# Graph attention passes of a GNN: values made beside the keys, selections made by VectorE, banks as accumulators

## The chip, the cores and the metric

The kernel runs on one core of a Trainium2 chip. The metric is the device time of one execution in microseconds; the kernel before takes 12023.37 us, the median of three runs from 12015.92 to 12034.72. The core has a matmul engine (TensorE, PE in profile rows; its weight loads are PEld), VectorE (DVE), ScalarE (ACT), GpSimd (POOL) and SyncE (SP), which only issues transfers and waits. Each runs its own instruction stream; they meet at semaphores.

## The reference, cut to what matters

Four graph layers run one after the other on 5000 nodes, 80000 edges sorted by destination, and width 128, all in float32. The first layer (`_L0_gnn_ref`) runs three times and holds all that is changed here:

```python
x_i = x[dst]
x_j = x[src] + edge_attr
q = (x_i @ wq.T + bq).reshape(-1, HEADS, DH)
k = (x_j @ wk.T + bk).reshape(-1, HEADS, DH)
v = (x_j @ wv.T + bv).reshape(-1, HEADS, DH)
alpha = jnp.sum(q * k, axis=-1) / jnp.sqrt(jnp.float32(DH))
a = softmax of alpha over the edges of one destination
out = jax.ops.segment_sum(a[..., None] * v, dst, num_segments=N)
```

The layer's remainder (a dense block, a GRU cell, norms) and the other three layers (neighbour sums with a two-layer net, four rounds of typed neighbour sums with a GRU, one more attention layer) are not touched.

## The kernel before, in words

Edges are taken in tiles of 128, nodes in 40 blocks of 128. A *step* is a pair (edge tile, node block) that the tile's destinations touch; there are 672 steps, planned at the start of the program (`step_tables`, lines 321 to 537: VectorE computes tables with one small operation after another, SyncE sends them through DRAM to where they are read into registers). Four steps make a *region* (`GROUP`), four regions a turn of a hardware loop (`REGIONS`, 42 turns). So a pass has 168 regions. `select` holds for a step a 128x128 matrix of zeros and ones: edge e belongs to node n of the block.

Each of the three rounds of the first layer has, among others:

- `gat_score_pass` (lines 986 to 1111). GpSimd gathers the rows `x[src]` of a region with four indirect DMAs (`gathers_by_step`, line 832; a gather may start once the region four places back is turned, `p_turned`). SyncE loads the edges' own rows into `attr`, four DMAs. VectorE builds `select` (line 862, edges down the partitions) and adds gathered rows and edge rows (line 1059). TensorE turns both: four transposes of `select` (line 1091), four of the sum (line 1093). ScalarE copies the two turned banks to SBUF (`spread`, line 1039; `mixT`, line 1040). SyncE stores `mixT` in DRAM (`rows_dram`, line 1024) for the value pass. TensorE makes the keys, `mixT` times `wk` (line 1105), and brings each edge the query of its destination, `spread` times the block's queries (line 1108). ScalarE copies the keys (line 1048), VectorE multiplies, sums by head and adds a bias term (lines 1068, 1073, 1076). Leads, in regions: VectorE's select and sum two ahead, TensorE's turning one ahead. PSUM: one bank each for the turned select and the turned sum, keys and queries with two buffers each.
- `gat_softmax`, not touched.
- `gat_value_pass` (lines 1113 to 1235). SyncE loads `rows_dram` back, one DMA for a region. TensorE makes the values from it with `wv` (line 1220). The selection is made by GpSimd (a difference, line 1144) and ScalarE (absolute value, line 1158, and 1 minus it, cut at zero, line 1161). VectorE weighs the values with the softmax weights (line 1171). TensorE sums the edges of each node (line 1231), and VectorE adds each step's 128x132 result to the accumulators in SBUF, steps by turns to `acc` and `t1` (lines 1188, 1190); at the end one addition joins the two (line 1212).

Other passes of the program matter for the rows below: `sum_pass` (lines 898 to 984) gathers by edge tile with a ring of 16 regions and sums in PSUM banks that are never copied in between; its banks are cleared first by eight matmuls (line 982).

## Time and profile before

| | us |
|---|---|
| median of three runs | 12023.37 |
| the profiled execution's own time | 12019.95 |
| its span, first to last instruction | 12018.1 |
| PE busy | 6550.1 |
| PEld busy | 5479.0 |
| POOL busy | 6209.6 |
| DVE busy | 4612.7 |
| ACT busy | 2251.5 |

Busy times are sums over the whole program, and the engines take turns in setting the pace, so they are read by stage: a window of the trace for each pass, then the groups of instructions and the waits in it. "Idle before" is the time that an engine sat idle ahead of a group's instructions; a releaser is what ended it ("issue": nothing that the profile shows; "remote": an event that it does not tie to an instruction).

### The profile page before, as it was taken

The numbers are of one execution on the slowest core, as the hardware profiler recorded it, in microseconds if no ns is written. First come the engines' busy times: TensorE is split into PE (matmuls) and PEld (weight loads), VectorE is DVE, ScalarE is ACT, GpSimd is POOL, SyncE is SP. The second block draws the span as 40 slices with busy tenths as digits, with TensorE's granted clock in tenths as the row PEclk, the third lists the DMA queues.
The fourth block names the chain that finished last, engine by engine and source line by source line (L and its number), as shares of the span: only waits on it lengthen the run. The fifth ranks groups of instructions, "written<-read, shape, count | busy, mean of one in ns | idle before, by whom it ended". The sixth has DMA issues, their size and how long they took to land. (4 is left out here: it accounts for less than half of the span.)

```text
span 12018.1 us, 148393 instructions
## 1 busy us (share of the span) xinstructions
PE 6550.1 (55%) x36272; PEld 5479.0 (46%) x36273; DVE 4612.7 (38%) x10118; ACT 2251.5 (19%) x4313; POOL 6209.6 (52%) x6365
## 2 busy tenths in 40 slices
PE   3666786566786665884335334433533443365555
PEld 3555665555765555853323223233323322244443
DVE  4444754444754444752113112211311221135555
ACT  1222552222542222641000000000000000011111
POOL 2666423666414665504663665466366456625553
PEclk6777898777897777996667666666766666677777
DMA  2444322444313443401111111211111121112221
GB/s 75 128 127 127 103 64 69 128 127 125 106 42 88 129 128 105 125 22 42 46 45 61 46 46 36 68 45 46 60 45 45 34 71 46 46 43 77 78 77 55
DMA packets 698434, 894.29 MB, mean 74 GB/s; under 512 B 148417, under 2 KB 443211, under 8 KB 698130
## 3 DMA queue, kind: packets, MB, share of 16 engines
q0 software_dynamic: 198368, 429.61, 13.6%
q1 hardware_dynamic: 498474, 461.96, 12.4%
q8 instruction: 51, 0.84, 0.0%
q14 instruction: 125, 1.02, 0.0%
q10 hardware_dynamic: 1416, 0.86, 0.0%
HBM read 698.72 MB, written 193.14 MB: 74 GB/s over the span
## 5 line engine op out<-in xcount | busy, mean ns | idle before, releaser
L857 POOL DMA_INDIRECT states<-table_typed,tile_idx x2512 | 2415.9, 962 | 1777.8 <-issue 721.2
L840 POOL DMA_INDIRECT states<-table_x,src_idx x2016 | 1980.1, 982 | 1862.7 <-POOLq L82 742.8
L979 PE MATMUL psum<-states,l_sums_select 128*128 x4480 | 905.5, 336 | 1729.7 <-issue 1696.3
L979 PEld LDWEIGHTS psum<-states,l_sums_select 128*128 128x128 f32 x4480 | 777.0, 244 | 1854.3 <-issue 1853.8
L961 DVE SCALAR_TENSOR_TENSOR l_sums_select<-dst_all,pair_start,iota_row 128x512 f32<-128x512 f32 x560 | 402.1, 749 | 2212.5 <-remote 1401.0
L1091 PE MATMUL psum<-ident,select 128*128 128x128 f32 x2016 | 418.3, 344 | 1199.3 <-DVE states L1059 723.4
L840 POOL DMA_INDIRECT l_pass_ring<-table_kv,src_idx x672 | 655.1, 975 | 658.9 <-DVE score L1312 286.3
L1068 DVE TENSOR_TENSOR states<-w,psum 128x512 f32<-128x512 f32 x504 | 345.2, 685 | 1544.0 <-ACT w L1048 969.0
L857 POOL DMA_INDIRECT states<-table_x,tile_idx x628 | 602.1, 959 | 626.2 <-POOLq L82 337.0
L979 PE MATMUL psum<-states,select 128*128 x2240 | 469.4, 348 | 808.8 <-issue 769.4
L944 ACT COPY t<-psum 128x512 f32<-128x512 f32 x50 | 29.3, 585 | 4534.1 <-PE psum L979 2586.3
L1091 PEld LDWEIGHTS psum<-ident,select 128*128 128x128 f32 x2016 | 297.9, 178 | 1263.5 <-DVE states L1059 567.3
L979 PEld LDWEIGHTS psum<-states,select 128*128 128x128 f32 x2240 | 404.7, 254 | 876.7 <-issue 876.0
L1144 POOL TENSOR_TENSOR w<-iota_row,dst_local 128x512 f32<-128x512 f32 x504 | 524.3, 1041 | 459.7 <-ACT select L1161 459.7
L1108 PE MATMUL psum<-t,l_scores_spread 128*128 x4032 | 675.2, 317 | 72.1 <-issue 71.6
L1105 PE MATMUL psum<-wt,l_scores_mixT 128*128 128x128 f32 x4032 | 713.5, 336 | 0.0
L1105 PEld LDWEIGHTS psum<-wt,l_scores_mixT 128*128 128x128 f32 x4032 | 672.1, 252 | 0.6 <-issue 0.2
L1108 PEld LDWEIGHTS psum<-t,l_scores_spread 128*128 128x128 f32 x4032 | 630.4, 233 | 75.8 <-issue 75.7
L961 DVE SCALAR_TENSOR_TENSOR select<-dst_all,pair_start,iota_row 128x512 f32<-128x512 f32 x280 | 200.2, 749 | 1035.7 <-remote 567.1
L1231 PE MATMUL psum<-l_values_msg,select 128*128 128x132 f32 x4032 | 549.5, 279 | 68.2 <-DVE l_values_msg L1171 68.2
L1048 ACT COPY w<-psum 128x512 f32<-128x512 f32 x504 | 300.5, 596 | 1355.7 <-remote 844.0
L1220 PE MATMUL psum<-wt,l_values_ring 128*128 128x128 f32 x4032 | 535.7, 277 | 15.4 <-DMA l_values_ring<-rows_dram 15.4
(357 smaller groups left out, 11997.4 us busy)
## 6 DMA issues: line engine op xcount, KB each, us to landing
states<-in_edge_attr_dram SPq DMA_DIRECT2D x2016, 64.0 KB
rows_dram<-l_scores_mixT SPq DMA_DIRECT2D x504, 256.0 KB
l_values_ring<-rows_dram SPq DMA_DIRECT2D x504, 256.0 KB
table_typed<-l_rows_rows SPq DMA_DIRECT2D x40, 1024.0 KB, 4.3
states<-table_typed,tile_idx POOLq DMA_INDIRECT x2512
states<-table_x,src_idx POOLq DMA_INDIRECT x2016
l_pass_ring<-table_kv,src_idx POOLq DMA_INDIRECT x672
table_x<-l_rows_rows SPq DMA_DIRECT2D x40, 256.0 KB, 2.3
```

What stands on the lines that cost most here:

```text
L840: pool.indirect_dma_start(out=ring[:, k % REGIONS, u, :], out_offset=None, in_=table, in_offset=at).then_inc(gathered[k % REGIONS], 16)
L857: pool.indirect_dma_start(out=ring[:, k % TILE_RING, u, :], out_offset=None, in_=table, in_offset=at).then_inc(gathered[k % REGIONS], 16)
L961: dve.scalar_tensor_tensor(out=picked(k), in0=dst_all[:, bass.ds(column, GROUP)].unsqueeze(2).broadcast_to([P, GROUP, P]), scalar=pair_sta ...
L979: ins = pe.matmul(to, picked(k)[:, u, :], rows, start=False, stop=True, skip_group_check=True)
L1048: act.copy(key[:, r % 2, :, :], keys(r)).then_inc(p_evacuated, 1)
L1068: dve.tensor_tensor(prod.rearrange("p (a b) f -> p a b f", a=2), key[:, r % 2, :, :].rearrange("p (a b) f -> p a b f", a=2), queries(r)[:, ...
L1091: pe.transpose(psum[:, 0, u * P:(u + 1) * P], select[:, r, u, :], ident[:])
L1105: pe.matmul(keys(r)[:, u, :], mixT[:, r, u, :], wt[:, WK, :], start=True, stop=True)
L1108: ins = pe.matmul(queries(r)[:, u // pair, u % pair, :], spread[:, r % 2, u, :], q, start=True, stop=True)
L1144: pool.tensor_tensor(away[:, r % 2, :, :], iota_row[:].unsqueeze(1).broadcast_to([P, GROUP, P]), dst_local[:, bass.ds(step_of(i, r), GROUP ...
L1220: ins = pe.matmul(values(r)[:, u, :], ring[:, r, u, :], wt[:, WV, :], start=True, stop=True)
L1231: ins = pe.matmul(sums(r, u), select[:, r, u, :], msg[:, r, u, :], start=True, stop=True)
```

## The change

In the score pass the keys and the values are made by one matmul for a step, 256 columns wide (`both`, the two weight matrices side by side). ScalarE copies the keys as before and the values into `kept`, and issues the store of `kept` to `rows_dram`. The turned selection is no longer transposed: at the start of the program the local destinations of all steps are stored in DRAM (`dst_dram`, a row of 512 for a region); ScalarE issues, for each region, a DMA that lays this row out on all 128 partitions (`wanted`, two buffers), and VectorE compares it with the partition's number (`iota_col`), which gives `select` with nodes down the partitions. The sum of gathered rows and edge rows goes to `mix`, where the edge rows were loaded. VectorE leads by three regions now, TensorE's turning by two with two banks; keys and values have two buffers of two banks, the queries one buffer. In the value pass VectorE makes the selection with one comparison, VectorE weighs three of a region's four steps and GpSimd the fourth and copies the weights; TensorE adds each step's result to its block's place in a PSUM bank (three blocks in a bank, 14 banks' worth in eight banks); ScalarE copies a bank out when its last region is done and clears it for reuse. The tables for that are made at the start of the program.

The start of the program:

```diff
+                        sp.dma_start(dst_dram.ap().rearrange("r (u p) -> (r u) p", p=P).rearrange("(c k) p -> k c p", k=ROW_K), loc_f).then_inc(s_row, 16)
+                    with nc.allow_non_contiguous_dma(reason="table of the values' columns, once"):
+                        sp.wait_ge(s_value, 1)
+                        sp.dma_start(value_dram.ap().rearrange("a (c k) -> k a c", k=ROW_K), value_i[:]).then_inc(s_row, 16)
+                        sp.wait_ge(s_row, 80)
+                        by_region = value_dram.ap().rearrange("a (g u) -> a g u", u=GROUP)
+                        sp.dma_start(value_plan[:, :, 0:GROUP], by_region[0:1, :, :]).then_inc(s_in, 16)
+                        sp.dma_start(value_plan[:, :, GROUP:], by_region[1:2, :, GROUP - 1:]).then_inc(s_in, 16)
...
+                    link(dve.tensor_scalar(bank_f[:, 0, :], block_f[:], 171.0, None, ALU.mult))
...
+                    for c in range(VALUE_BANKS):
+                        link(dve.tensor_scalar(bank_f[:, 0, :], block_f[:], float(BANK_VALUES * (c + 1)) if c + 1 < VALUE_BANKS else float(BLOCKS + 1),
+                                               None, ALU.is_lt))
+                        link(dve.tensor_reduce(counts[:, c:c + 1], bank_f[:, 0, :], AX_X, ALU.add))
+                    dve.sem_inc(s_value, 1)
```

The score pass, engine by engine:

```diff
                     def _(sp):
                         def load(i, r):
-                            at_least(sp, p_mixed, region_of(i, r) - (REGIONS - 1))
+                            at_least(sp, p_turned, number(i, r) - (REGIONS - 1))
...
+                        def want(i, r):
+                            at_least(act, p_selected, number(i, r) - 1)
+                            act.dma_start(wanted[:, r % 2, :, :].rearrange("p u f -> p (u f)"),
+                                          dst_dram[bass.ds(number(i, r), 1), :].partition_broadcast(P)).then_inc(p_wanted[r % 2], 16)
+
                         def turned(i, r):
-                            act.wait_ge(p_turned, region_of(i, r) + 1)
-                            if not (isinstance(i, int) and i == 0):
-                                act.wait_ge(p_out[r], i * 16)
-                            at_least(act, p_projected, region_of(i, r) - 1)
-                            act.copy(spread[:, r % 2, :, :], bank4(psum[:, 0, :]))
-                            act.copy(mixT[:, r, :, :], bank4(psum[:, 1, :])).then_inc(p_spread, 1)
+                            act.wait_ge(p_turned, number(i, r) + 1)
+                            at_least(act, p_keyed, number(i, r) - (REGIONS - 1))
+                            act.copy(mixT[:, r % REGIONS, :, :], bank4(turned_rows(r))).then_inc(p_spread, 1)
 
                         def body(i):
-                            for r in range(REGIONS):
-                                if nxt := led(i, r, 1):
+                            for r in range(SCORE_RING):
+                                if nxt := ahead(i, r, 4):
+                                    want(*nxt)
+                                if nxt := ahead(i, r, 2):
                                     turned(*nxt)
...
+                                act.copy(in_pairs(key[:, r % 2, :, :]), made(r)[:, :, :, 0:D]).then_inc(p_evacuated, 1)
+                                if not (isinstance(i, int) and i == 0 and r < REGIONS):
+                                    act.wait_ge(p_out[r % REGIONS], uses(i, r) * 16)
+                                act.copy(in_pairs(kept[:, r % REGIONS, :, :]), made(r)[:, :, :, D:2 * D]).then_inc(p_valued, 1)
+                                act.wait_ge(p_valued, number(i, r) + 1)
+                                act.dma_start(rows_dram[bass.ds(number(i, r), 1), :, :].rearrange("a p (u f) -> (a p) u f", f=D),
+                                              kept[:, r % REGIONS, :, :]).then_inc(p_out[r % REGIONS], 16)
...
                         def lead(i, r):
-                            at_least(dve, p_turned, region_of(i, r) - (REGIONS - 1))
-                            make_select(dve, i, r)
...
+                            at_least(dve, p_projected, number(i, r) - (REGIONS - 1))
+                            dve.wait_ge(p_wanted[r % 2], (i * (SCORE_RING // 2) + (r // 2 + 1)) * 16)
+                            dve.tensor_scalar(select[:, r % REGIONS, :, :], wanted[:, r % 2, :, :], iota_col[:], None,
+                                              ALU.is_equal).then_inc(p_selected, 1)
+                            dve.wait_ge(gathered[r % REGIONS], landed(uses(i, r), base[r % REGIONS]))
+                            dve.wait_ge(p_in[r % REGIONS], (uses(i, r) + 1) * (16 * GROUP))
+                            dve.tensor_tensor(mix[:, r % REGIONS, :, :], ring[:, r, :, :], mix[:, r % REGIONS, :, :], ALU.add).then_inc(p_mixed, 1)
...
                         def turn(i, r):
...
-                            for u in range(GROUP):
-                                pe.transpose(psum[:, 0, u * P:(u + 1) * P], select[:, r, u, :], ident[:])
...
+                                at_least(pe, p_valued, j - 1)
                                 for u in range(GROUP):
-                                    pe.matmul(keys(r)[:, u, :], mixT[:, r, u, :], wt[:, WK, :], start=True, stop=True)
+                                    ins = pe.matmul(made(r)[:, u // pair, u % pair, :], mixT[:, r % REGIONS, u, :], both, start=True, stop=True)
+                                ins.then_inc(p_keyed, 1)
+                                at_least(pe, p_score_kept, j)
                                 for u in range(GROUP):
                                     q = t1[:, bass.ds(blocks[u] * Q_W, Q_W)]
-                                    ins = pe.matmul(queries(r)[:, u // pair, u % pair, :], spread[:, r % 2, u, :], q, start=True, stop=True)
+                                    ins = pe.matmul(queries[:, u // pair, u % pair, :], select[:, r % REGIONS, u, :], q, start=True, stop=True)
```

The value pass (the memsets, the projection, the three selection operations and the additions of before are gone):

```diff
                     def _(pool):
...
+                                pool.tensor_copy(msg[:, r, :, D:W], weights)
+                                pool.wait_ge(p_in[r], (i + 1) * 16)
+                                pool.tensor_tensor(msg[:, r, SHARE:, 0:D].rearrange("p u (h e) -> p u h e", h=GAT_HEADS),
...
                     def _(dve):
...
+                                make_select(dve, i, r)
+                                dve.wait_ge(p_in[r], (i + 1) * 16)
+                                dve.tensor_tensor(msg[:, r, 0:SHARE, 0:D].rearrange("p u (h e) -> p u h e", h=GAT_HEADS),
...
                     def _(act):
+                        done = by_step(act, value_done, 0, VALUE_BANKS, STEPS // GROUP, 1)
+                        for c in range(VALUE_BANKS):
+                            n = min(BANK_VALUES, BLOCKS - c * BANK_VALUES)
+                            act.wait_ge(p_summed, done[c])
...
+                            if c + 8 < VALUE_BANKS:
+                                act.wait_ge(p_drained, c + 1)
+                                act.activation(psum[:, c % 8, :], none, ACT.Copy, scale=0.0).then_inc(p_cleared, 1)
...
                     def _(pe):
...
+                                entries = by_step(pe, value_row, j * (GROUP + 1), GROUP + 1, 8 * CHUNK)
+                                pe.wait_ge(p_cleared, entries[GROUP].with_bounds(min_val=1, max_val=VALUE_BANKS))
+                                pe.wait_ge(p_selected, j + 1)
+                                pe.wait_ge(p_weighted, j + 1)
+                                pe.wait_ge(p_weight, j + 1)
                                 for u in range(GROUP):
+                                    to = banks[:, bass.ds(entries[u].with_bounds(min_val=0, max_val=8 * CHUNK - W), W)]
+                                    ins = pe.matmul(to, select[:, r, u, :], msg[:, r, u, :], start=False, stop=True, skip_group_check=True)
                                 ins.then_inc(p_summed, 1)
+                        for bank in range(8):
+                            ins = pe.matmul(psum[:, bank, :], blank[:], ones[0:1, 0:1].broadcast_to([1, CHUNK]), start=True, stop=True)
```

## Rows read from the trace of the kernel before

**Rows 1.** The cores view: span and mean granted TensorE clock.

```profile
core 0: 12018.1 us, clock 0.734
```

**Rows 2.** Windows: busy us of PE PEld DVE ACT POOL, clock, DMA share, GB/s.

```profile
203.40:1256.30 1052.90, 635.16 (x4032) 612.45 (x4032) 470.85 (x840) 269.16 (x504) 660.97 (x672) 0.77 0.43 126
...
1316.00:1664.60 348.60, 314.48 (x2688) 306.39 (x2688) 270.43 (x1012) 233.04 (x506) 179.34 (x169) 0.98 0.45 127
```

**Rows 3.** Groups by line, 300 to 1200 us: busy, mean, idle before, releasers.

```profile
L840 POOL DMA_INDIRECT states<-table_x,src_idx x584 | 575.5, 985 | 326.2 <-issue 166.0 <-remote 145.1 <-PE psum L1093 15.0
L1105 PE MATMUL psum<-wt,l_scores_mixT 128*128 128x128 f32 x1168 | 206.5, 336 | 0.0
...
L1091 PE MATMUL psum<-ident,select 128*128 128x128 f32 x584 | 122.3, 347 | 335.2 <-DVE states L1059 225.2 <-ACT l_scores_mixT L1040 76.2 <-issue 33.7
...
L862 DVE TENSOR_TENSOR select<-iota_row,dst_local 128x512 f32<-128x512 f32 x145 | 100.4, 693 | 22.7 <-issue 13.4 <-PE psum L1093 4.9
...
L1068 DVE TENSOR_TENSOR states<-w,psum 128x512 f32<-128x512 f32 x145 | 99.3, 685 | 440.5 <-ACT w L1048 277.0 <-issue 163.4
```

**Rows 4.** Source view of the gathers: ns min/median/max, first and last start.

```profile
L840 POOL DMA_INDIRECT states<-table_x,src_idx x672: 938/945/1470, 204.0 to 1236.0; - x168
...
L857 POOL DMA_INDIRECT states<-table_x,tile_idx x628: 939/945/1446, 5495.8 to 6386.2; - x157
```

**Rows 5.** Timeline, 406.8 to 407.4 us: start us, us, engine, line.

```profile
406.83 0.69 DVE L1059 TENSOR_TENSOR states<-states 128x512 f32<-128x512 f32 x1
406.90 1.43 POOL L840 DMA_INDIRECT states<-table_x,src_idx  x1 [0.31 <-issue]
```

**Rows 6.** Timeline, 381 to 396 us, all engines.

```profile
381.15 1.07 PE L1108 MATMUL psum<-t,l_scores_spread 128*128 x8
...
386.63 0.27 PE L1108 MATMUL psum<-t,l_scores_spread 128*128 x1 [0.95 <-issue]
...
392.43 0.59 ACT L1048 COPY w<-psum 128x512 f32<-128x512 f32 x1 [8.97 <-remote]
...
393.29 0.94 POOL L840 DMA_INDIRECT states<-table_x,src_idx  x1 [2.97 <-remote]
```

**Rows 7.** Timeline of SyncE alone, 381 to 400 us.

```profile
387.32 4.97 SPq L1017 DMA_DIRECT2D states<-in_edge_attr_dram  x4
...
395.89 1.98 SPq L1017 DMA_DIRECT2D states<-in_edge_attr_dram  x4
```

**Rows 8.** Timeline: a transfer issued by ScalarE; VectorE at 82 us.

```profile
1.18 0.44 ACTq L243 DMA_DIRECT2D wn<-in_L_gnn_w_ao_dram  x1
...
82.67 0.62 DVE L411 CAST t<-src_i 96x896 f32<-96x896 int32 x1 [9.94 <-DMA dst_i<-in_dst_dram,tile_i]
```

**Rows 9.** Source view: a one-input operation, the clearing matmuls, the last addition.

```profile
L717 DVE TENSOR_SCALAR l_rows_xs<-states x20: 362/418/428, 173.6 to 1948.1; 128x512 f32 x12, 128x512 f32<-128x512 f32 x8
...
L982 PE MATMUL psum<-ones,blank x80: 1056/1056/1188, 5495.2 to 9694.0; 1*128 1x512 f32 x80
...
L1212 DVE TENSOR_TENSOR states<-states,t x3: 5657/5657/5658, 1658.9 to 5168.1; 128x5280 f32<-128x5280 f32 x3
```

**Rows 10.** DMA queues, 300 to 1200 us: packets, MB, share of 16 engines.

```profile
q1 hardware_dynamic: 104688, 76.40, 26.8%
q0 software_dynamic: 18656, 38.24, 16.9%
```

**Rows 11.** Windows again, one microsecond in the start of a value pass.

```profile
1321.20:1322.20 1.00, 1.00 (x6) 1.00 (x7) 1.00 (x1) 0.00 (x0) 1.00 (x2) 0.50 1.00 381
```

**Rows 12.** Groups by line, 1330 to 1655 us, inside a value pass.

```profile
L1231 PE MATMUL psum<-l_values_msg,select 128*128 128x132 f32 x1307 | 178.4, 279 | 21.7 <-DVE l_values_msg L1171 21.7
L1220 PE MATMUL psum<-wt,l_values_ring 128*128 128x128 f32 x1304 | 171.8, 275 | 0.0
L1144 POOL TENSOR_TENSOR w<-iota_row,dst_local 128x512 f32<-128x512 f32 x162 | 168.6, 1041 | 151.5 <-ACT select L1161 151.5
...
L1171 DVE TENSOR_TENSOR l_values_msg<-psum,l_values_msg 128x256 f32<-128x256 f32 x327 | 135.6, 415 | 0.0
```

More of the change, by code:

```diff
@@ L998, in gat_score_pass, with turned_rows @@
                 pair = GROUP // 2
-                def keys(r):
-                    return bank4(psum[:, 2 + r % 2, :])
-                def queries(r):
-                    return psum[:, 4 + 2 * (r % 2):6 + 2 * (r % 2), 0:pair * Q_W].rearrange("p a (b w) -> p a b w", w=Q_W)
-                with block(name, p_selected, p_mixed, p_turned, p_spread, p_projected, p_evacuated, p_multiplied, p_scored,
-                           p_score_kept, *p_in, *p_out) as b:
+                def turned_rows(r):
+                    return psum[:, r % 2, :]
@@ new lines, in made, with in_pairs, ring_turns @@
+                def made(r):
+                    return psum[:, 2 + 2 * (r % 2):4 + 2 * (r % 2), :].rearrange("p a (b w) -> p a b w", w=2 * D)
+                def in_pairs(ap):
+                    return ap.rearrange("p (a b) f -> p a b f", b=pair)
+                queries = psum[:, 6:8, 0:pair * Q_W].rearrange("p a (b w) -> p a b w", w=Q_W)
+                def ring_turns(eng, body):
+                    body(0)
+                    with eng.Fori(1, SCORE_TURNS - 1) as i:
+                        body(i)
+                    body(SCORE_TURNS - 1)
@@ new lines, in ahead, with number, first_step, uses @@
+                def ahead(i, r, lead):
+                    i2, r2 = i + (r + lead) // SCORE_RING, (r + lead) % SCORE_RING
+                    return None if isinstance(i2, int) and i2 >= SCORE_TURNS else (i2, r2)
+                def number(i, r):
+                    return i * SCORE_RING + r
+                def first_step(i, r):
+                    return i * (SCORE_RING * GROUP) + r * GROUP
+                def uses(i, r):
+                    return i * (SCORE_RING // REGIONS) + r // REGIONS
@@ L1049, in _ @@
+                        for r in range(4):
+                            want(0, r)
                         turned(0, 0)
-                        turns(act, body)
+                        turned(0, 1)
+                        ring_turns(act, body)
                     @b.vector
@@ L1214, in _ @@
                     @b.tensor
                     def _(pe):
-                        def project(i, r):
-                            pe.wait_ge(p_in[r], (i + 1) * 16)
-                            at_least(pe, p_weighted, (region_of(i, r) - (REGIONS - 1)) * 2)
-                            for u in range(GROUP):
-                                ins = pe.matmul(values(r)[:, u, :], ring[:, r, u, :], wt[:, WV, :], start=True, stop=True)
-                            ins.then_inc(p_projected, 1)
                         def body(i):
```

214 lines of the change are left out of this document (97 added, 117 removed).

## The prediction

> **What bounds the kernel now.** I read the span and clock first [rows 1]: 12018.1 us of one core, TensorE at a mean granted clock of 0.734. Then I cut the trace into the stages that the diff touches. One window for the first score pass and one for the first value pass [rows 2] show two stages: a score pass takes 1053 us and comes three times, a value pass 349 us, three times too. Together about 4205 (3 x 1402) of 12018 us; nothing else is changed but the tables at the start. Each pass has 168 regions, so a region costs 6.27 us in a score pass and 2.07 us in a value pass.
>
> In the score pass no compute engine is full: PE is busy 635 of 1053 us at clock 0.77, DVE 471, ACT 269 [rows 2]. The groups by line [rows 3] show the pace-maker: GpSimd's gathers take 985 ns each, and its idle time is the smallest part of its stretch. The best that it can do stands in the source view [rows 4]: the median gather is 945 ns, and 0.30 us lie between two of a run [rows 5], so four cost 4.98 us, a pass 837 us. It takes 1033 us (204.0 to 1236.0 plus the last), 1.537 us a gather, 6.15 a region, and about 20 us after the last gather. The difference, 1.17 us a region, has two sources. One is small: a gather that starts while VectorE runs an operation with two SBUF inputs is late, 1.43 us where 0.945 is usual [rows 5]. The large one is in the timeline [rows 6]: eight records of L1108 take 1.07 us at 381.15, but from 386.63 on the same records come one by one, 0.7 to 2.1 us apart, SyncE's four issues take 4.97 us where 1.98 is usual [rows 7], ScalarE waits 8.97 us for an event, and at 393.29 the gathers have waited 2.97 us, since their ring of four regions is full. I call this the crawl. It hits PE and SP while gathers follow one another closely and ends after the gathers stop. What causes it no row tells. A pass with the same gathers, a ring of 16 regions and fewer other transfers needs 891 us for 628, 1.42 each, 5.68 for four [rows 4]. So 4.98 is the floor, 5.68 the best seen, 6.15 the present.
>
> **The score pass, part by part.** PE: four select transposes go, 122.3 us over 146 regions, 0.84 a region; the key matmuls double their columns, +206.5/146 = 1.41 [rows 3]. Net +0.57, from 635/168 = 3.78 to 4.35 us a region at the present clock mix. That stays under 5.68, but PE is no relief.
>
> ACT: copies stay three (spread goes, the values come). Two transfer issues a region are new, at 0.44 us each [rows 8]: 1.60 + 0.88 = 2.5 us, under 5.7, hidden while PE and the gathers work. Behind an issue stand the copy of the turned rows and the key copy, and VectorE waits for the latter, 277 us in the chain "DVE L1068 <- ACT" today, the most frequent releaser [rows 3]. If the cover goes, all of the 0.88 is on the path.
>
> DVE: the selection was a two-input operation, 693 ns [rows 3]; now it has one tensor input. The nearest row is 418 ns, 0.36 to 0.43 [rows 9]. Gain 0.27, DVE 2.80 to 2.53 us; not a bound.
>
> SP: one issue of five goes, and with it the wait for `p_spread` ahead of the next loads; its 64 KB loads can only come earlier.
>
> The chain: queries of region j-2, key copy, multiply, reduce, bias, select, sum, turning of j+1, keys, queries of j. It spans two regions. The key copy now lies before the queries (-0.60), the selection is shorter (-0.27), the query buffer is single, but lead and turning both move one region ahead, so the distance is the same; PE's turning and keys cover the 1.6 us of VectorE for which the single query buffer waits. -0.87 for two regions, -0.43 for one: 6.15 - 0.43 = 5.72, close to 5.68, which I see as the mark that gathers under such disturbance reach.
>
> DMA: a fourth 256 KB a region. Today the queues hold 26.8 + 16.9 = 43.7% of 16 engines [rows 10] at 6.2 us a region, 2.7 us of engine time; a 256 KB read of 2 KB rows adds about 0.7 (one microsecond at full share moved 381 KB [rows 11]), so 3.4 of 5.7 us, 60%. Hidden. But the new load reads one row 128 times and is asked for one region ahead, which no row shows: between -0 and, if it arrives a region late, the waits of rival 4.
>
> I take 5.8 us a region, 5.72 plus 0.08 for longer gathers while there are more of these operations in the run. Ends: 5.0 (the floor) and 6.4 (PE's added 0.57 unhidden, less the chain's gain, plus part of the issues). Gain a pass: 168 x (6.15 - 5.80) = 59 us; three: 176.
>
> A rule speaks against this edit. First the row: only VectorE operations with two SBUF inputs are seen beside gathers, and they delay one by up to 0.48 us [rows 5]. The Trainium skill, "SBUF — State Buffer", section "Who interferes with whom", says that a one-input copy or tensor_scalar in a two-port mode takes the port pair that VectorE shares with GpSimd for the whole instruction, so that GpSimd can't write descriptors meanwhile; "VectorE: DVE Perf Modes" has float32 tensor_scalar from SBUF in that mode, and the 418 ns for 512 columns [rows 9] agrees. By it the new selection holds gathers where the old one only held the read. That is rival 3.
>
> **The value pass.** Inside it a region takes 325/163 = 1.99 us [rows 12]; 348.6 - 168 x 1.99 = 14 us are start and end, 5.66 of them the last addition [rows 9]. PE is the bound, clock 0.98, with 178.4 + 171.8 us of 325. Now:
> - PE: the projection goes, -171.8/163 = 1.05; 1.09 left, plus a read of five table entries which its queue takes while it computes.
> - DVE: additions go; selection 0.69 as L862 [rows 3], weighing of 384 columns 0.55 (between 0.415 for 256 [rows 12] and 0.69 for 512): 1.24.
> - POOL: 1041 ns for 512 columns [rows 12] makes 0.26 for 128, and a copy of 16 columns, I say 0.14: 0.40.
> - ACT: only 14 bank copies and 6 clears a pass, beside the rest.
> - SP's loads: 256 KB at 381 GB/s is 0.7 us [rows 11], hidden, four buffers.
>
> Both operations of VectorE and both of GpSimd read SBUF. If they take turns, as in rows 5, a region costs 1.24 + 0.40 = 1.64; if not, 1.24. The nearest row is the 1.43 us gather, which did wait, so I take 1.65. PE would then be busy 66% of the time; in the score pass it is 60% busy and its clock averages 0.77 (2.4 GHz for part, 1.2 GHz for the rest), and at 1.2 GHz its 1.09 becomes near 2.0. So the upper end is 2.0, the lower 1.24. Start: the two memsets go, eight clearing matmuls of 1.056 us at most come [rows 9], 8.5; the last addition becomes one bank copy of 0.6. 13 us. Pass: 168 x 1.65 + 13 = 290, gain 59; three: 176. Ends: 221 and 349, gains of 127 and 0.
>
> **Tables.** 37 small VectorE operations at about 0.2 us, 7.6 us, stand ahead of a wait of 9.94 us for gathered indices [rows 8]: hidden. Three more small transfers in the chain that VectorE awaits later: +3 us, between 0 and 10.
>
> **Sum.** 12018.1 - 176 - 176 + 3 = 11669; with the 1.9 us around the span (own time 12019.95) 11671, and the median of the runs lies 3 us above that execution: 11,670 us is said.
>
> **Rivals.**
> 1. Both passes run at their floors: score 5.1 us a region (176 a pass), value 1.3 (117). For it: leads are longer, PE and ACT lose the select turning. Against: gathers with 16 regions of room reach only 5.68. 3 x 293 less: 11,145.
> 2. The score pass doesn't move: the crawl, not the chain, makes the 1.17 us, and PE's +0.57 eats the -0.43. For it: waits of 9 us are no chain of 0.6 us copies. Only the value pass gains: 11,845.
> 3. The selection holds the gathers: 0.42 us in each region on top of my 5.8, 168 x 0.42 x 3 = 212: 11,880. Against: DVE has the choice of 0.30 us gaps.
> 4. Slower: ScalarE crawls. It now issues two transfers a region in the stretches in which SP's four took 4.97 us instead of 1.98 [rows 7]. All that waits for its copies waits too, and the gathers behind. One more such 5 us for each turn of four regions is 42 x 5 = 210 us a pass; 12,020 + 630 - 174 = 12,475. It decides from 59/42 = 1.4 us a turn on, where it eats the value pass's gain.
>
> **How the numbers follow.** Forecast 0.40, rival 1 0.15, rival 2 0.22, rival 3 0.09, rival 4 0.10, nothing moves 0.04. The likeliest one's own range is 11,450 to 11,830. The range of 8 in 10 takes in rivals 2 and 3 and half of 1: 11,200 to 12,000. 0.2%, 24 us, is about what a measurement of this kernel tells from no change (its runs spread by 19). Faster 0.86, within 0.03, slower 0.11.
>
> **What would show it.** Right: the score pass near 980 us and 1.45 us a gather; the selection near 0.42 us; the value pass near 290 us with GpSimd's operations longer than 0.26 us where VectorE is in one; PE busy less and at a lower clock there. Wrong: gathers above 1.1 us in most regions (rival 3); waits for `wanted` ahead of the selection, or ScalarE's issues of over 1 us (rival 4); PE as the releaser of everything in the value pass at 1.2 GHz. It is wrong as a whole if the score pass is longer than 1053 us or the value pass is under 220.

## The result: 0.3% slower, and the profile after

The changed kernel takes 12057.76 us, the median of eight runs (12043.39 to 12071.24), against 12021.37 us of the kernel before in eight runs of its own (12014.27 to 12034.72). The ratio is 1.003, with a 95% interval of 1.0019 to 1.004: slower by about 36 us, where 350 us less were forecast.

The same windows as in [rows 2], for the changed kernel: us, busy us of PE, PEld, DVE, ACT and POOL, granted clock, DMA share, GB/s. The first is the first score pass, the second the first value pass.

```profile
209.40:1265.90 1056.50, 709.63 (x3360) 617.35 (x3360) 444.12 (x840) 271.09 (x504) 649.61 (x672) 0.79 0.59 167
...
1328.00:1681.90 353.90, 242.29 (x1360) 200.76 (x1360) 196.66 (x336) 10.23 (x20) 231.03 (x336) 0.87 0.44 125
```

Neither stage became shorter. The three score passes take 1056.5, 1052.5 and 1055.7 us, 7 more than before in sum; the value passes 353.9, 354.6 and 354.4, 16 more; the tables 6 more (the first gather starts at 210.0 us, before at 204.0 [rows 4]). The rest of the 47 us between the two spans lies in stages that are the same code in both, some a few us shorter, some longer. The first score pass is longer than 1053 us, which the prediction named as the sign that it is wrong as a whole.

The gathers of that score pass, in the source view, answer to [rows 4]: number, min/median/max ns, first and last start.

```profile
L888 POOL DMA_INDIRECT states<-table_x,src_idx x672: 942/947/1467, 210.0 to 1240.9; - x168
```

1.535 us a gather where it was 1.537. The parts of the pass moved the way that was priced, if by less: TensorE is busy 709.63 us instead of 635.16, +0.44 us a region (0.57 priced), and VectorE 444.12 instead of 470.85, -0.16 (0.27 priced). The pace did not move. Groups by line, 300 to 1200 us of the changed kernel, as [rows 3]:

```profile
L888 POOL DMA_INDIRECT states<-table_x,src_idx x583 | 562.6, 965 | 338.3 <-issue 171.9 <-remote 163.1 <-PE psum L1178 3.3
L1190 PE MATMUL psum<-wt,l_scores_mixT 128*128 128x256 f32 x1166 | 340.6, 444 | 0.0
...
L1155 DVE TENSOR_TENSOR states<-w,psum 128x512 f32<-128x512 f32 x146 | 100.3, 687 | 454.9 <-issue 300.5 <-ACT w L1123 154.2
...
L1123 ACT COPY w<-psum 128x512 f32<-128x512 f32 x146 | 86.0, 589 | 353.1 <-remote 171.7 <-PE psum L1190 168.5 <-issue 13.0
...
L1141 DVE TENSOR_SCALAR select<-l_scores_wanted,iota_col 128x512 f32<-128x512 f32 x146 | 72.7, 498 | 33.1 <-issue 20.2 <-DMA l_scores_wanted<-dst_dram 8.4
```

The gathers became shorter (985 to 965 ns) and sat idle longer instead (326.2 to 338.3 us). The timeline shows for what. Changed kernel, 410 to 418 us: start us, us, engine, line, and in brackets the idle time before it and what ended it.

```profile
410.33 1.06 PE L1195 MATMUL psum<-t,select 128*128 x8
...
411.23 0.60 PE L1178 MATMUL psum<-ident,l_scores_mix 128*128 128x128 f32 x4
...
414.08 0.94 POOL L888 DMA_INDIRECT states<-table_x,src_idx  x1 [0.30 <-issue]
...
416.82 0.69 DVE L1155 TENSOR_TENSOR states<-w,psum 128x512 f32<-128x512 f32 x1 [6.68 <-issue]
416.89 0.59 ACT L1113 COPY l_scores_mixT<-psum 128x512 f32<-128x512 f32 x1 [3.39 <-remote]
...
417.59 0.95 POOL L888 DMA_INDIRECT states<-table_x,src_idx  x1 [2.57 <-remote]
```

TensorE's turning of the rows is recorded at 411.23 to 411.83, in the middle of a run of eight gathers. The gather at 417.59 waits for exactly that turning, ScalarE's copy of the turned rows too (it starts at 416.89). VectorE waits for TensorE's queries (recorded up to 411.4) and for ScalarE's copy of the keys (recorded up to 413.0). All three go on 1.8 to 2.6 us after the last gather of the run has ended, over 5 us after TensorE's records. I call it the hold. Over the first pass, the gathers resume after 83 gaps of 2.39 us (median), 4.40 us after the record of the last turning ahead of them; in the kernel before, 81 gaps of 2.15 us, 5.00 us after it. A gap comes once in eight gathers (2 x 4.98 + 2.4 = 12.3 us for two regions, as measured) in both kernels.

The value pass is told by one row of the source view of the table reads (PEldq is TensorE's sequencer), which had no counterpart on TensorE before:

```profile
L923 PEldq TENSOR_LOAD <-value_plan x168: 584/1234/1254, 1328.1 to 1678.8; - x168
```

and by the groups inside it, 1345 to 1670 us, as [rows 12]:

```profile
L1279 PE MATMUL psum<-l_values_msg,select 128*128 128x132 f32 x1284 | 217.6, 323 | 107.9 <-DVE select L910 81.5 <-issue 18.4 <-POOL l_values_msg L1233 6.8
...
L1231 POOL COPY l_values_msg<-score 128x16 f32 x161 | 115.0, 714 | 111.0 <-PE psum L1279 111.0
L1233 POOL TENSOR_TENSOR l_values_msg<-l_values_ring,score 128x128 f32<-128x128 f32 x161 | 114.9, 713 | 0.0
L910 DVE TENSOR_TENSOR select<-iota_row,dst_local 128x512 f32<-128x512 f32 x161 | 113.1, 702 | 145.0 <-PE psum L1279 144.4
```

VectorE and GpSimd wait for TensorE, though its matmuls fill 218 of 325 us. Between them stands the read of five table entries: 1.23 us in three regions of four and 0.58 in the fourth. The granted clock is not the pace, though it is lower than before (0.87, before 0.98): in 45 regions the eight matmul records take over 1.5 us instead of 1.16, and from the start of such a region to that of the next 2.00 us pass on average, in the other regions 2.04.

### The profile page after: what moved, and what is told of

Read it like the earlier page. It is cut to its first block and busy times, and to the rows that moved or that the text cites. A ratio compares the mean times of both kernels' runs of the same rounds, so it can differ in the third digit from the quotient of the medians.

```text
span 12065.2 us, 132651 instructions
## 1 busy us (share of the span) xinstructions
PE 6587.4 (55%) x30274; PEld 5186.4 (43%) x30275; DVE 4326.0 (36%) x8135; ACT 1593.9 (13%) x2861; POOL 6350.0 (53%) x6867
## 5 line engine op out<-in xcount | busy, mean ns | idle before, releaser
L888 POOL DMA_INDIRECT states<-table_x,src_idx x2016 | 1953.4, 969 | 1881.3 <-POOLq L87 736.1
L1195 PE MATMUL psum<-t,select 128*128 x4032 | 735.0, 339 | 963.7 <-DVE score L1163 561.7
L1190 PE MATMUL psum<-wt,l_scores_mixT 128*128 128x256 f32 x4032 | 1183.3, 446 | 0.3
L1195 PEld LDWEIGHTS psum<-t,select 128*128 128x128 f32 x4032 | 664.5, 240 | 1081.1 <-issue 1065.2
L1190 PEld LDWEIGHTS psum<-wt,l_scores_mixT 128*128 128x128 f32 x4032 | 905.3, 237 | 152.7 <-issue 13.4
L1279 PE MATMUL psum<-l_values_msg,select 128*128 128x132 f32 x4032 | 687.4, 324 | 332.5 <-DVE select L910 240.1
L1279 PEld LDWEIGHTS psum<-l_values_msg,select 128*128 128x128 f32 x4032 | 589.0, 222 | 434.8 <-issue 433.2
L1231 POOL COPY l_values_msg<-score 128x16 f32 (+1 forms) x504 | 357.8, 710 | 590.1 <-PE psum L1279 340.3
L910 DVE TENSOR_TENSOR select<-iota_row,dst_local 128x512 f32<-128x512 f32 (+1 forms) x840 | 496.4, 591 | 444.5 <-PE psum L1279 441.5
L1178 PE MATMUL psum<-ident,l_scores_mix 128*128 128x128 f32 x2016 | 416.1, 344 | 77.0 <-issue 64.8
```

The lines of the kernel that those rows point to most:

```text
L888: pool.indirect_dma_start(out=ring[:, k % REGIONS, u, :], out_offset=None, in_=table, in_offset=at).then_inc(gathered[k % REGIONS], 16)
L910: eng.tensor_tensor(select[:, r, lo:lo + n, :], iota_row[:].unsqueeze(1).broadcast_to([P, n, P]), dst_local[:, bass.ds(step_of(i, r, lo), ...
L1178: ins = pe.transpose(turned_rows(r)[:, u * P:(u + 1) * P], mix[:, r % REGIONS, u, :], ident[:])
L1190: ins = pe.matmul(made(r)[:, u // pair, u % pair, :], mixT[:, r % REGIONS, u, :], both, start=True, stop=True)
L1195: ins = pe.matmul(queries[:, u // pair, u % pair, :], select[:, r % REGIONS, u, :], q, start=True, stop=True)
L1231: pool.tensor_copy(msg[:, r, :, D:W], weights)
```

## The experiments

The kernel before ran beside each on the same chip; its median is given. In all of them a register that a wait uses is held at 0 or above, one register operation a wait. The time of a score pass is that of the layer's first round, from the first gather to the last instruction (by that count the kernel before has 1052 us and the changed one 1056; the expectations count from the first selection, 3 us less). The kernels came to chips of two kinds (last section): where the kernel before took 12,010 to 12,110 us there was the hold, where it took about 10,645 there was none. "..." in a diff marks lines left out, here above all those of the register bound.

**aligned_read** (value pass; its table laid out so that four places start at a multiple of four entries)

```diff
-entries = by_step(pe, value_row, j * (GROUP + 1), GROUP + 1, 8 * CHUNK)
+entries = by_step(pe, value_row, j * GROUP, GROUP, 8 * CHUNK) + by_step(pe, value_row, j + STEPS, 1, 8 * CHUNK, 0, [0])
```

> The changed kernel, with the value pass's table laid out so that a region's four places start at a multiple of four entries and its bank number is read by itself; nothing else of the passes. (Here and in all kernels below a register that a wait uses is first held at 0 or above, one register operation a wait, the same in every one.) Theory (TensorE's register read sets the pace): the trace of the changed kernel shows reads of five entries that take 0.59 us in every fourth region, where they start at a multiple of four, and 1.24 us in the other three, in TensorE's own sequence between the matmuls of two regions; the two reads now take 0.33 + 0.25 us, so a region falls from 2.03 to about 1.5 us, where GpSimd's two operations of 0.71 each take over: a value pass 354 -> 270 us, the kernel 12058 -> 11805. Rival (VectorE and GpSimd, which hold each other up at SBUF, set the pace): value pass within 5 us of 354 and no change.

Measured: 12055.46 us, before 12108.63; ratio 0.9955 (0.994 to 0.9971). The value pass takes 327 us. The reads, as in the source view above:

```profile
L923 PEldq TENSOR_LOAD <-value_plan x336: 298/325/352, 1351.9 to 1677.0; - x168
```

The fair comparison is not 354 but 371 us: that is what a pass takes in freed_by_sum, pause_by_region and plain_loads, with the same bound on the register and the old table (371 to 372 us in all seven such runs, on three chips). One register operation a region costs 17 us a pass, 0.10 us a region. So TensorE's own sequence is the pace, as the theory has it. The size was missed (327 us, not 270): two reads, 0.33 and 0.31 us, still stand between the matmuls of two regions.

**freed_by_sum**, **pause_by_region**, **plain_loads** (score pass)

```diff
-gathers_by_step(pool, ring, table_x[:], p_turned)
+gathers_by_step(pool, ring, table_x[:], p_mixed)
```

> The changed kernel, with the score pass's gathers allowed to start when VectorE has read their slot (the sum has left the ring) instead of when TensorE has turned the sum. Theory G (runs of gathers hold back TensorE's and SyncE's events, and the pace is eight gathers and one gap of 2.5 us): VectorE's sums of the next regions themselves wait for TensorE's queries, so the gaps stay, a pass within 15 us of 1056, the kernel within 45 us of 12058. Rival C (the chain of copies, sums and turnings sets the pace): the gathers are freed about 2 us earlier in each turn of the chain, 6.14 -> about 5.7 us a region, a pass 1056 -> 980, the kernel about 11830.

```diff
+                at_least(pool, p_weight, k)
+                pool.memset(spare, 0.0).then_inc(p_weight, 1)
```

> The changed kernel, with one GpSimd memset of 128x300 (about 0.3 us, with its start about 0.55) after each region's four gathers in the score pass. Theory G: if a pause of that size lets TensorE's and SyncE's events through, the gaps of 2.5 us vanish and a region takes 4 x 1.245 + 0.55 = 5.55 us, a pass 935 us, the kernel about 11700; if the hold-up needs longer to end, the memset comes on top of the gaps, 6.7 us a region, a pass near 1140, the kernel about 12320. Rival C (the gathers only wait for the chain): the memset runs in the time in which GpSimd waits anyway (2.4 us in two regions against 1.1), so a pass within 15 us of 1056.

```diff
-                        gathers_by_step(pool, ring, table_x[:], p_turned)
...
+                            for u in range(GROUP):
+                                sp.dma_start(ring[:, r, u, :], table_x[(4 * r + u) * P:(4 * r + u + 1) * P, :]).then_inc(p_in[r % REGIONS], 16)
```

> The changed kernel, with the score pass's gathers replaced by plain transfers of the same size: SyncE loads fixed rows of the node table, 4 x 64 KB a region, beside the edges' own rows, so the rows of the sources are not the gathered ones; GpSimd does nothing in the score pass. Theory G: TensorE and SyncE no longer crawl, and the pace is that of SyncE's eight issues at about 0.52 us or of TensorE, 4.1 to 4.7 us a region: a pass 700 to 790 us. Rival C (the chain through TensorE, ScalarE and VectorE needs 6 us a region by itself): a pass over 1000 us.

Measured, all beside 12108.63 us of before, where a score pass of aligned_read is 1077 us: freed_by_sum 12545.17 us (ratio 1.0362, 1.0333 to 1.0391), a pass of 1189 us; pause_by_region 12196.91 us (1.0071, 1.0053 to 1.0088), a pass of 1076 us; plain_loads 11435.18 us in a single run, 820 us from the first selection. The source view of the gathers in freed_by_sum and then in pause_by_region:

```profile
L888 POOL DMA_INDIRECT states<-table_x,src_idx x672: 939/945/1469, 211.8 to 1373.3; - x168
```

```profile
L888 POOL DMA_INDIRECT states<-table_x,src_idx x672: 940/947/1436, 211.9 to 1262.6; - x168
```

Rival C's forecast of 76 us less is refuted by the first: the gathers were given more freedom, and the pass became 112 us longer. They no longer wait for the turning but for VectorE's sum, and resume 0.81 us (median) after its record. It is the sum that comes late, and the gaps are 4.1 us long. The hold lies ahead of it: ScalarE's copy of the turned rows starts 4.0 us after the record of the turning, against 2.8 in pause_by_region on the same chip (means of the first pass's 168 regions). Theory G failed too in its number (no more than 15 us): I had not thought that freedom could hurt. In pause_by_region neither half of G came true: the pause vanished in the gaps, as C said; it neither ended the hold nor came on top. plain_loads came close to G: the same bytes without gathers leave no hold (ScalarE's copy starts 0.4 us after the turning, at most 1.3), and nothing else needs more than 4.9 us a region. VectorE's sums wait there for SyncE's loads to land, 217 of 700 us.

**two_gathers**, **no_edge_loads**, **keys_alone** (score pass; who pays for the hold)

```diff
-                for u in range(GROUP):
+                for u in range(n):
...
-                        gathers_by_step(pool, ring, table_x[:], p_turned)
+                        gathers_by_step(pool, ring, table_x[:], p_turned, 2)
```

> The changed kernel, with two gathers for a region of the score pass instead of four; the other two steps' rows are what the ring held. Theory G2 (TensorE's and SyncE's instructions and events are slow only while gathers are under way, and the chain itself needs at most the 4.9 us of plain_loads): half the gather time halves the 1.3 us lost to them: about 5.2 us a region, a pass about 890 us (1074 with four on the chip of plain_loads, 820 with none). Rival C (GpSimd's 4.98 us for four gathers plus a fixed wait of 1.2 us is the pace): 2.5 + 1.2, bounded by the chain, 4.9 or less, a pass 800 to 830.

```diff
-                        ring_turns(sp, body)
+                        for r in range(SCORE_RING):
+                            load(0, r)
...
-                            dve.wait_ge(p_in[r % REGIONS], (uses(i, r) + 1) * (16 * GROUP))
+                            if isinstance(i, int) and i == 0:
+                                dve.wait_ge(p_in[r % REGIONS], (uses(i, r) + 1) * (16 * GROUP))
+                            at_least(dve, p_turned, number(i, r) - (REGIONS - 1))
```

> The changed kernel, without SyncE's loads of the edges' rows after the first four regions: a sum is added to what the buffer held. SyncE is idle and the transfers are a third fewer. Theory G2 with TensorE as the one held back: a region stays within 0.2 us of 6.2, a pass over 1020 us. Rival S (SyncE's four issues, which take 2 us alone and up to 10 us beside gathers, are what the sums wait for): under 5.8 us a region, a pass under 975.

```diff
...
-ins = pe.matmul(made(r)[:, u // pair, u % pair, :], mixT[:, r % REGIONS, u, :], both, start=True, stop=True)
+ins = pe.matmul(made(r)[:, u // pair, u % pair, 0:D], mixT[:, r % REGIONS, u, :], wt[:, WK, :], start=True, stop=True)
```

> The changed kernel, with the keys alone in the score pass's matmuls, 128 columns instead of 256, and the keys stored where the values would be: the same number of instructions, 1.4 us a region less work on TensorE by the rows of the kernel before. Theory G2 (what counts is instructions and events of TensorE's sequence, not its columns): a pass falls by less than 30 us. Rival P (the doubled columns are on the path, and ate what the shorter chain gave): 6.2 -> 5.4 us or less, a pass under 950 us.

Beside 12012.57 us of before, one run each: 10856.1, 12078.82 and 12108.22 us; a score pass with all of its work takes 1052 us on this chip (turn_read). The gathers of the three, in the order above:

```profile
L888 POOL DMA_INDIRECT states<-table_x,src_idx x336: 939/946/1457, 211.2 to 827.3; - x168
```

```profile
L888 POOL DMA_INDIRECT states<-table_x,src_idx x672: 938/944/1466, 210.9 to 1231.2; - x168
```

```profile
L888 POOL DMA_INDIRECT states<-table_x,src_idx x672: 939/945/1448, 210.0 to 1240.2; - x168
```

Without SyncE's loads a pass takes 1041 us, with half of the columns in the key and value matmuls 1050 us: the loads cost at most 11 us of the pass and the columns 2, and rivals S and P are out. With two gathers it takes 638 us, 3.80 us a region, below both numbers on record. The total alone does not tell the theories apart: 6.26 - 3.80 = 2.46 us a region is what two gathers cost (2.49), as if a fixed wait had stayed, and C's own 2.5 + 1.2 us without its bound of the chain would be near. The trace does. The window of 300 to 800 us in two_gathers, as in [rows 2]:

```profile
300.00:800.00 500.00, 468.60 (x2712) 388.53 (x2711) 358.58 (x677) 223.41 (x405) 277.41 (x272) 1.00 0.83 249
```

TensorE is busy 469 of 500 us at a granted clock of 1.00, so its own work is now the pace, where it was busy 710 of 1056 us in the changed kernel, at a granted clock of 0.79. The gathers resume 1.05 us after the turning that frees them, a plain chain. In the kernels with four gathers that wait for the turning it is 4.2 us or more on chips with the hold (medians of the first pass). ScalarE's copy starts over 2 us after the turning in 6 of the 168 regions; with four gathers on chips with the hold it does in 79 to 88 of them, in plain_loads and on chips without the hold in none. So runs of gathers hold TensorE's events, and the chain by itself needs at most 3.8 us. On a chip with the hold the pace is not the work, but the coming through of TensorE's events.

**turn_read** (value pass; places and bank numbers read once for four regions)

```diff
...
+places = by_step(pe, value_row, step_of(i, 0), REGIONS * GROUP, 8 * CHUNK)
+gates = by_step(pe, value_row, region_of(i, 0) + STEPS, REGIONS, 8 * CHUNK, 0, range(REGIONS))
```

> The changed kernel, with the value pass's places and bank numbers read once for a turn of four regions: sixteen places that start at a multiple of four entries, and four bank numbers. In aligned_read TensorE's sequence issues without a pause from one region to the next, 1.77 us: two reads of 0.33 and 0.31 us and what lies around them. Theory (that sequence is the pace): the reads fall to about 1.1 + 0.34 us for four regions, 0.36 a region instead of 0.87 with what lies around, so TensorE needs 1.3 us, and GpSimd's two operations of 0.71 us (1.43) or VectorE's 1.24 take over: a value pass 327 -> 260 us. Rival (GpSimd and VectorE already pace aligned_read): a value pass over 315.

Measured: 11679.68 us, before 12012.57; ratio 0.9719 (0.9703 to 0.9735): the version that beats both kernels. A value pass takes 227.7 us instead of 371. The reads (four bank numbers 0.33, sixteen places 1.11 us), and the groups by line, 1345 to 1550 us:

```profile
L923 PEldq TENSOR_LOAD <-value_plan x84: 328/720/1123, 1326.7 to 1549.3; - x84
```

```profile
L1286 PE MATMUL psum<-l_values_msg,select 128*128 128x132 f32 x1290 | 155.8, 279 | 48.7 <-DVE select L910 47.3 <-ACT psum L1270 1.2 <-issue 0.2
...
L910 DVE TENSOR_TENSOR select<-iota_row,dst_local 128x512 f32<-128x512 f32 x162 | 142.7, 881 | 0.3 <-PE psum L1286 0.3
L1238 POOL TENSOR_TENSOR l_values_msg<-l_values_ring,score 128x128 f32<-128x128 f32 x161 | 114.8, 713 | 0.0
L1236 POOL COPY l_values_msg<-score 128x16 f32 (+1 forms) x162 | 106.5, 657 | 0.0
L1253 DVE TENSOR_TENSOR l_values_msg<-l_values_ring,score 128x384 f32<-128x384 f32 x161 | 87.8, 545 | 0.0
```

Now VectorE (0.3 us) and GpSimd (0.0) have no idle time, and TensorE waits for VectorE's selection. A region takes 205/162 = 1.27 us, less than I had expected: the records of VectorE's two operations (881 and 545 ns) overlap by 0.08 us at each end, and GpSimd's overlap too; the sum of their durations is not a pace.

**deep_ring**, twice (turn_read with eight regions of room), **vector_weighs** (turn_read with all four steps weighed by VectorE)

```diff
-SCORE_RING = REGIONS
+SCORE_RING = 2 * REGIONS
...
-                        gathers_by_step(pool, ring, table_x[:], p_turned)
+                        gathers_by_step(pool, ring, table_x[:], p_turned, SCORE_RING, base)
```

> turn_read with a gather ring of eight regions instead of four in the score pass (the products are written over the keys and the values have two buffers instead of four, to make room; a gather still waits for the turning of the region that was in its place). In all runs with four gathers a region and four regions of room, the turning that a gather waits for is recorded 4.2 to 4.8 us before the gather starts, and the gaps are 2.3 to 2.5 us, once in eight gathers; with two gathers it is 1.05 us. Theory H (the event comes through only after a run of gathers ends, one gap for each time that the ring fills): eight more gathers before the ring is full, runs of 16 and gaps of 2.5 to 4 us: 1.40 to 1.49 us a gather, a pass 960 to 1015 us against 1049, the kernel 11420 to 11580. Rival K (TensorE and what follows it are slow for as long as gathers run, so more room only lengthens their slow time): 1.53 us a gather or more, as in freed_by_sum, a pass of 1045 us or more, the kernel at 11680 or above.

```diff
-            SHARE = GROUP - 1
+            SHARE = GROUP
...
-                                pool.tensor_copy(msg[:, r, :, D:W], weights)
...
+                                pool.tensor_copy(msg[:, r, :, D:W], weights).then_inc(p_weight, 1)
```

> turn_read with VectorE weighing all four steps of a region in the value pass, GpSimd only copying the 16 weights. In turn_read a value pass takes 227 us inside its accumulation, 1.29 us a region, and GpSimd's two operations of 0.66 and 0.71 us beside VectorE's 0.69 and 0.55. Theory (the two engines take turns at SBUF, so the small GpSimd operation costs what it costs beside VectorE, and VectorE's 0.69 + 0.69 is now the sum): 1.38 to 1.45 us a region, a pass 232 to 244 us, the kernel 11695 to 11730. Rival (GpSimd's 1.37 us is the pace of turn_read and goes away): TensorE's 1.2 to 1.3 us takes over, a pass at or under 220 us, the kernel at or under 11660.

Both fell on a chip without the hold: the kernel before took 10644.74 us there. deep_ring 10315.76 us (0.9692, 0.9676 to 0.9708), vector_weighs 10293.57 us (0.9669, 0.9653 to 0.9686), with score passes of 876 and 874 us. The gathers, with eight regions of room and with four:

```profile
L891 POOL DMA_INDIRECT states<-table_x,src_idx x672: 940/944/1451, 210.3 to 1072.0; - x168
```

```profile
L888 POOL DMA_INDIRECT states<-table_x,src_idx x672: 940/944/1457, 211.2 to 1071.0; - x168
```

1.28 us a gather with either, near the 1.245 of a run without a pause: the ring makes no difference where there is no hold, and whether it does where there is one was not seen. The value pass takes 225.7 us with VectorE alone and 228.5 with the shared work (deep_ring), between the two numbers on record; the intervals of the two ratios overlap. So who carries that quarter matters little, and VectorE's groups in vector_weighs, 1165 to 1370 us, show why:

```profile
L910 DVE TENSOR_TENSOR select<-iota_row,dst_local 128x512 f32<-128x512 f32 x163 | 111.4, 683 | 5.5 <-PE psum L1281 0.9
L1248 DVE TENSOR_TENSOR l_values_msg<-l_values_ring,score 128x512 f32<-128x512 f32 x163 | 111.1, 681 | 0.0
```

Without GpSimd's product beside it the selection takes 0.68 us instead of 0.88, which pays for the longer weighing (0.68 instead of 0.55). VectorE has next to no idle time in both and is the pace in both, 1.26 and 1.27 us a region.

> The kernel of deep_ring once more. deep_ring and vector_weighs ran on a chip on which the kernel before took 10645 us instead of 12012 to 12109, and on which the gathers ran at 1.28 us each in both, at four and at eight regions of room: there the hold-up of TensorE's events did not exist, and deep_ring could not tell its theories apart. If this run falls on a chip with the hold-up (the kernel before near 12000): theory H (one gap for each filling of the ring) says 1.40 to 1.49 us a gather, a score pass of 960 to 1015 us; rival K (TensorE is slow for as long as gathers run) says 1.53 us a gather or more, 1045 us or more. If it falls on a chip without it, a pass of 872 us as before, and nothing is told apart.

> The changed kernel itself, with only the registers that waits use held at 0 or above, which adds one register operation a region to TensorE's sequence in the value pass. By pause_by_region against the changed kernel's own trace that operation costs 371 - 354 = 17 us a value pass, 50 in all. On a chip with the hold-up: score passes within 10 us of the kernel before's, the kernel 1.003 x before + 50 us, a ratio of 1.006 to 1.009. On a chip without it: the gathers' floor holds in both kernels, score passes of 872 us, the ratio the value pass's: 3 x (371 - 349) + 6 = 72 us over 10645, 1.006 to 1.008. Rival (without the hold-up the shorter chain and fewer late gathers count after all, or TensorE's doubled columns do): a ratio under 1.002, or over 1.012.

Both came to such a chip again, and the first stays inconclusive: 10300.69 us (0.9675, 0.9659 to 0.9692). changed_bound takes 10725.72 us, before 10643.65; ratio 1.0075 (1.0058 to 1.0092), as expected: 3 x 22 us in the value passes (371 us, against 349 in the trace of the kernel before, which is from a chip with the hold) and 6 in the tables make 72 of the 82 us. Its gathers, and one turning with its followers in the timeline, 408 to 409.1 us:

```profile
L888 POOL DMA_INDIRECT states<-table_x,src_idx x672: 940/944/1457, 209.9 to 1067.6; - x168
```

```profile
408.02 0.66 PE L1183 MATMUL psum<-ident,l_scores_mix 128*128 128x128 f32 x4 [0.93 <-DVE l_scores_mix L1150]
...
408.79 0.59 ACT L1118 COPY l_scores_mixT<-psum 128x512 f32<-128x512 f32 x1 [1.48 <-PE psum L1183]
...
409.09 0.94 POOL L888 DMA_INDIRECT states<-table_x,src_idx  x1 [0.30 <-issue]
```

ScalarE's copy starts 0.1 us after the turning, and the gathers never stop.

## Why the prediction was wrong

**Which step failed.** Two terms of 176 us, both gone. In the value pass it is the clause "plus a read of five table entries which its queue takes while it computes": priced at nothing, it is the pace. The read takes 1.23 us, and it stands in TensorE's sequence between two regions' matmuls, and with what lies around it a region needs 2.0 us where I had 1.65. This is shown: aligned_read and turn_read change this read alone and give 44 and 143 us a pass, and a single register operation costs 17. With turn_read the pass is 62 us shorter than my 290, so the other terms were, if anything, too dear. The Trainium skill, "Runtime: NRT & Kernel Launch", section "Instruction fetch mechanics", gives the runtime's own loads of registers, from HBM, about 200 ns a register even in bulk; this table lies in SBUF, so it is only the nearest figure there, and I had not weighed it. By it the five are an estimated 1.0 us; the trace shows 1.23 from most starts, but only 0.33 us for four and 0.58 for five that start at a multiple of four.

In the score pass it is "I take 5.8 us a region": that the chain's -0.43 us reaches the gathers. Rival 2, which let the crawl rather than the chain make the 1.17 us, had the pass itself right to 4 us and carried 0.22. Its sentence "waits of 9 us are no chain of 0.6 us copies" was the one to follow; my "mark" of 5.68 came from another pass with a ring four times as deep. What the rival had wrong is that TensorE's +0.57 mattered (keys_alone: it does not). Whether the chain became 0.43 us shorter at all no run shows; the runs show that it does not set the pace. On a chip without the hold there was no gain to be seen either: of the 82 us by which changed_bound is slower than the kernel before, 72 are the value passes and the tables; the kernel before has no trace there.

**The smaller steps.** DMA share 0.60 forecast, 0.59 measured. ScalarE's issues 0.34 and 0.36 us where I had 0.44, and no crawl on it: rival 4 did not happen. The new selection takes 486 ns (median) instead of 418. Rival 3, by which it would hold the gathers for its whole length, is out too: counted in the trace, 60 gathers of a pass start inside it and have a median of 1056 ns, those inside the two-input operations of before 1122 and 1130, those inside operations that read PSUM 945; gathers over 1.1 us fell from 73 to 24 a pass. The gathers of the first pass take 649.6 us instead of 661.0, a gain of 11 us, which the gaps took back. By the Trainium skill, "SBUF — State Buffer", section "Who interferes with whom", a one-input operation in a two-port mode locks GpSimd out for its whole length; by that rule a gather would be up to 0.49 us late, and the 0.11 us of the median say that few were. In the value pass GpSimd's copy of 16 columns takes 714 ns (196 at its shortest) and its 128 columns 713, 1.43 instead of my 0.40; it did not decide only because the read did. The clearing is 16 matmuls, 14 us, where I counted 8: [rows 9] has 80 for five passes. Tables +6 us, within my 0 to 10.

**What stays open.** Why runs of gathers hold TensorE's events, on some chips only; and whether a deeper ring pays under the hold. It does not end the hold by itself: the later passes have a ring of 16 regions, and on chips with the hold they take 1.42 to 1.44 us a gather, on the others 1.26 to 1.27.

## What to carry to other kernels

A register read from a table is work in its engine's own sequence: count it between the last instruction of one step and the first of the next, read many entries at once, and let them start at a multiple of four. Before a shorter chain is credited, look whether the waiting engine starts soon after the record of what it waits for; where it is released by an event recorded long ago (here 4 to 5 us), the chain is not the pace. A larger freedom for the engine that does the holding can cost time (112 us a pass in freed_by_sum).

## What the runs showed of the hardware

Chips differ: the same kernel before took 12,013 and 12,109 us on two and 10,645 and 10,644 on others. The traces of the changed kernel and its variants show that nearly all of the difference lies in the passes with gathers: a score pass 1052 to 1077 us or 872 to 877, a pass of the later layers (628 gathers, a ring of 16 regions) at 1.42 to 1.44 or 1.26 to 1.27 us a gather, while a value pass took 371 us on both kinds.

Reads of table entries into registers cost 0.31 us for one, 0.33 for four and 1.11 for sixteen that start at a multiple of four. Five cost 0.58 us from such a start and 1.23, 0.25 each, from any other.

The value pass's selection (VectorE, 128x512, two inputs in SBUF) took 881 ns on average in turn_read, beside GpSimd's product of two SBUF inputs, and 683 in vector_weighs, without it.
